# Layer 3 of a four-layer kernel: the next batch's group norm one step earlier, and keys' means between those of the first queries

## What is computed

```python
qkv = silu(x @ w_qkv.T)                     # q, k, v, each 8 heads of 32
q = rope(rms_norm(q, w_qn)); k = rope(rms_norm(k, w_kn))
wp = silu(x @ w_wp.T + b_wp)                # a width and a sharpness per head and position
scores = q . k over a 7x7 window * scale    # k and v zero-padded
soft_mask = sigmoid((width - rel_dist) * sharp)
attn = softmax(scores - (1 - soft_mask) * 10000)
out = rms_norm(sum(attn * v_window), w_on)
return silu((out + v) @ w_out.T)
```

## Time and profile before

| | us |
|---|---|
| median of 3 runs | 3466.73 (3464.69 to 3476.52) |
| the profiled execution, whole time | 3469.34 |
| its span on the core | 3467.5 |
| TensorE matmul busy | 3105.6 (90% of the span) |
| VectorE busy | 2211.7 (64%) |
| ScalarE busy | 2058.1 (59%) |
| GpSimd busy | 1155.1 (33%) |

### The profile page before, as it was taken

How to read it: one execution, slowest core, us unless ns; L and a number is a source line. 1 busy time by engine, 2 the same in 40 slices (tenths; PEclk the granted TensorE clock), 3 DMA queues, 4 the chain that set the end, 5 groups by cost and what they waited for, 6 DMA issues and landing times. The chain is left out here.

```text
span 3467.5 us, 94027 instructions
## 1 busy us (share of the span) xinstructions
PE 3105.6 (90%) x38656; PEld 1750.2 (50%) x38656; DVE 2211.7 (64%) x5202; ACT 2058.1 (59%) x4412; POOL 1155.1 (33%) x1446
## 2 busy tenths in 40 slices
PE   6999999999955999999999858999994899999996
PEld 2333333333312556566656526777772566666664
DVE  5878878887733667676777533545543566666765
ACT  2667676767633555545555515656562677777774
POOL 3433434343301222222222202222222455555554
PEclk9999999999976999999999979999997999999998
DMA  6777787777852333323323214445443233333332
GB/s 201 155 173 164 157 184 173 152 174 160 170 130 68 66 86 84 83 72 86 84 71 72 74 57 139 145 143 159 145 133 128 67 93 107 107 113 113 110 95 83
DMA packets 286233, 413.94 MB, mean 119 GB/s; under 512 B 25952, under 2 KB 242800, under 8 KB 264816
## 3 DMA queue, kind: packets, MB, share of 16 engines
q1 hardware_dynamic: 263248, 270.32, 26.0%
q0 software_dynamic: 18432, 134.23, 19.4%
q10 hardware_dynamic: 4128, 3.39, 0.3%
HBM read 219.30 MB, written 53.81 MB: 79 GB/s over the span
## 5 line engine op out<-in xcount | busy, mean ns | idle before, releaser
L732 DVE TENSOR_TENSOR l_probs<-l_psum,l_decay 128x1024 f32<-128x1024 f32 x512 | 598.6, 1219 | 163.5 <-PE l_psum L628 152.8
L780 ACT ACTIVATE l_sizes<-l_probs 128x2048 f32<-128x2048 f32 x256 | 487.6, 1910 | 300.3 <-DVE l_probs L732 293.0
L1793 ACT ACTIVATE l_logits<-l_logits,l_low 128x100 f32<-128x100 f32 x1024 | 374.7, 369 | 238.1 <-DVE l_low L1773 237.1
L1800 POOL TENSOR_TENSOR l_logits<-l_logits,l_inv 128x400 f32<-128x400 f32 x256 | 235.0, 918 | 737.7 <-DVE l_inv L1779 736.8
L628 PE MATMUL l_psum<-l_qk 32*128 32x512 f32 x2048 | 340.6, 646 | 7.9 <-POOL l_qk L866 4.2
L881 POOL DMA_DIRECT2D l_sizes<-l_sizes x128 | 111.5, 871 | 548.1 <-ACT l_sizes L780 536.1
L1632 POOL TENSOR_TENSOR l_E<-l_E,l_causal 128x1024 f32<-128x1024 f32 x64 | 153.3, 2396 | 378.0 <-DVE l_x_act L1365 224.8
L643 PE MATMUL l_psum<-l_probs,l_V 128*32 128x512 f32 x2048 | 270.6, 600 | 1.7 <-DVE l_probs L732 1.6
L299 PE MATMUL l_psum<-l_xT,l_w_up 128*128 128x512 f32 x512 | 232.2, 607 | 12.7 <-DVE l_row_var L1423 8.6
L1735 PE MATMUL l_psum<-l_keys,l_q_blocks 128*64 128x100 f32 x4096 | 230.6, 253 | 3.7 <-issue 2.4
L2726 POOL TENSOR_SCALAR l_soft<-l_dist,l_sharp,l_border 128x100 f32<-128x100 f32 x512 | 229.0, 464 | 0.1
(11 more groups left out here) (246 smaller groups left out, 6072.0 us busy)
## 6 DMA issues: line engine op xcount, KB each, us to landing
l_sizes<-l_sizes POOLq DMA_DIRECT2D x128, 1024.0 KB, 7.5
l_V_windows<-v_image SPq DMA_DIRECT2D x512, 100.0 KB
l_V_windows<-v_padded SPq DMA_DIRECT2D x512, 100.0 KB
l_E<-rows_c SPq DMA_DIRECT2D x64, 512.0 KB, 5.8
l_xT<-y SPq DMA_DIRECT2D x24, 1024.0 KB, 5.3
y<-l_res SPq DMA_DIRECT2D x32, 512.0 KB, 3.7
l_e_everywhere<-rows_e SPq DMA_DIRECT2D x112, 128.0 KB, 5.6
l_xT<-x SPq DMA_DIRECT2D x8, 1024.0 KB, 11.7
```

The lines of the kernel that those rows point to most:

```text
L732: nc.vector.tensor_tensor(probs[:, N % 2, 2 * p:2 * p + 2, :], ring.region(name).rearrange("p (a n) -> p a n", a=2), decay[:, h:h + 2, s0: ...
L780: nc.scalar.activation(sizes[:, slot(N), :, :], probs[:, N % 2, :, :], ACT.Abs).then_inc(sized, 1)
L1793: nc.scalar.activation(e, e, ACT.Exp, scale=-1.0, bias=self.low[:, N % 4, i:i + 1], accum_out=self.total[:, N % 4, i:i + 1]).then_inc(self ...
L1800: nc.gpsimd.tensor_tensor(p, p, self.inv[:, N % 4, :].unsqueeze(2).to_broadcast([P, STEP, NKEY]), ALU.mult).then_inc(self.p_ready, 1)
```

## The change

- In `MEANS` the first key's mean comes between those of the first two queries, and a table `MEAN_OF` tells where a unit's mean is. VectorE scales key 0 in step 13 instead of 14, key 1 in step 14 instead of 15, keys 2 and 3 in step 15 as before; query 1 is scaled in step 14 as before.
- `bn_stats` of the first half of batch b+2 run in step 15 of batch b, ahead of that step's keys (those of batch b+1 were in step 0). Those of the second half and the combining are in step 0 (were in step 1). For the first transition, all of it is in step 0.
- The group average, its copy, the variance and the root are in step 1 (were in step 2). In the ring, `("gn", b + 1)` thus stands ahead of the last values' transpose.
- GpSimd applies the norm in step 2 (was step 3), again behind that step's scaling.

```diff
-MEANS = (("q", 0, 0), ("q", 0, 1), ("k", 0), ("k", 1), ("k", 2), ("k", 3), ("q", 1, 0), ("q", 1, 1))
+MEANS = (("q", 0, 0), ("k", 0), ("q", 0, 1), ("k", 1), ("k", 2), ("k", 3), ("q", 1, 0), ("q", 1, 1))
+MEAN_OF = {("q", u): (0, 2, 6, 7)[u] for u in range(4)} | {("k", u): (1, 3, 4, 5)[u] for u in range(4)}
-KEYS_AT = {14: (0, 1), 15: (1, 4)}
+KEYS_AT = {13: (0, 1), 14: (1, 2), 15: (2, 4)}
...
-            if n == 2 and b + 1 < B:
+            if n == 1 and b + 1 < B:
                 order.append(("gn", b + 1))
...
-                    if n == 2 and b + 1 < B:
+                    if n == 1 and b + 1 < B:
                         norm.average(nc, pe, ring, b + 1)
...
-                    if n < 2 and b + 1 < B:
-                        norm.moments_of(nc, dve, b + 1, n)
+                    if n == 15 and b + 2 < B:
+                        norm.moments_of(nc, dve, b + 2, 0)
+                    if n == 0 and b + 1 < B:
+                        if b == 0:
+                            norm.moments_of(nc, dve, 1, 0)
+                        norm.moments_of(nc, dve, b + 1, 1)
+                        norm.combine(nc, dve, vstep)
                     if n == 1 and b + 1 < B:
-                        norm.combine(nc, dve, vstep)
-                    if n == 2 and b + 1 < B:
                         norm.collect(nc, dve, ring, b + 1)
...
-                            scale_query(b + 1, n - 13)
+                            scale_query(b + 1, 2 * (n - 13))
...
-                    if n == 2 and b + 1 < B:
+                    if n == 1 and b + 1 < B:
                         norm.root(nc, act, b + 1)
...
-                    if b + 1 < B and n == 2:
+                    if b + 1 < B and n == 1:
                         norm.variance(nc, pool, pstep, ring, b + 1)
                     if b + 1 < B:
-                        if n == 3:
+                        if n == 2:
                             apply(b + 1)
```

More of the change, by code:

```diff
@@ L2142 @@
 SQUARES_AT = {10: (0, 2), 11: (2, 3), 12: (3, 4), 13: (4, 6), 14: (6, 8)}
-KEYS_AT = {14: (0, 1), 15: (1, 4)}
+KEYS_AT = {13: (0, 1), 14: (1, 2), 15: (2, 4)}
 def number_of(j):
-    return j - 2 if MEANS[j][0] == "k" else j if j < 2 else j - 4
+    return sum(MEANS[i][0] == MEANS[j][0] for i in range(j))
 def unit_name(unit, b):
@@ L2474, in scale_key @@
                     g, half = u % 2, u // 2
-                    dve.wait_ge(r_ready, 8 * b + u + 3)
+                    j = MEAN_OF["k", u]
+                    dve.wait_ge(r_ready, 8 * b + j + 1)
                     r0 = WIN // 2 + 16 * half
                     k = keys[b % 2][:, g, :].rearrange("p (r c) -> p r c", c=IMAGE)[:, r0:r0 + 16, WIN // 2:WIN // 2 + SIDE]
-                    nc.vector.scalar_tensor_tensor(k, k, w_qk[:, 0:1], rec[:, (u + 2) % 4, :].rearrange("p (r c) -> p r c", c=SIDE),
+                    nc.vector.scalar_tensor_tensor(k, k, w_qk[:, 0:1], rec[:, j % 4, :].rearrange("p (r c) -> p r c", c=SIDE),
                                                    ALU.mult, ALU.mult).then_inc(k_done, 1)
```

## The result

The changed kernel takes 3490.22 us (median of 12 runs, 3477.44 to 3494.43) beside 3471.41 us for the kernel before in the same comparison (12 runs, 3455.25 to 3485.89): a ratio of 1.0050, with a 95% interval of 1.0031 to 1.0069. That is slower by 0.5%, some 17 to 19 us. The forecast was 3479.5 us, 12.8 above the median then known (3466.73).

The account below looks back on a forecast made before the run. TensorE, busy 92 of 100 us, bounds the kernel, so the change acts only through its stalls. Six steady transitions at 1.8 us plus 1.7 for the first give 12.5 us more: 3479.5 us, range 3464 to 3491.

Parts of the forecast that it names:

- the main case: The whole kernel slower through the added stalls, 3475 to 3486 us; chance 0.62.
- the case with the clock: Rival: two stalls within 7 us lower TensorE's clock, 1.8 to 3 us more a transition, about 3497 us; chance 0.08.
- Item 1: VectorE's interleaved keys, steps 13 to 15: same work up to step 0, cost and gain 0.
- Item 2: First bn_stats pair ahead of step 15's keys: TensorE's stall before step 0's scores grows from 0.47 to 1.7, +1.2 us.
- Items 3 and 4: Steps 0 and 1: VectorE's scores start later; the group average waits 1.9 us for ScalarE's copy of a value transpose.
- Items 5 and 6: From the average to step 4: +2.6 us at the outputs' mean, +1.8 at the step-4 units without the norm's wait.
- item 5: From the average to the outputs' mean (L2381): 6.74 us of TensorE work, ScalarE ends last at 2921.8; shift +2.6 us.
- Item 7: GpSimd's scaling for step 4's turn, now behind the apply: just in time, price 0; starved, up to 0.8 us late.
- The first transition: No keys to delay, but both pairs and the combining precede step 1's scores: step-4 units +1.7 us.
- Half of it swallowed: Rival: the step-5 stall on the values takes back half of the shift, leaving 6 us, 3473 us; chance 0.23.

Follow-up runs that it names:

- e1: The kernel before with the interleaved order of means and keys alone: six batch periods 545.29 us, against 545.03 before.
- e2: The kernel before with only the first bn_stats pair moved to step 15, ahead of the keys: six periods 552.26 us, against 545.03 before.
- e4: The changed kernel with TensorE's group average at the end of step 1, behind turn and weighing: six periods 547.55 us, against 560.44.
- e3: The changed kernel with the bn_stats pair of step 15 behind that step's keys instead of ahead: six periods 554.81 us, against 560.44.
- e6: The changed kernel with GpSimd's apply of the norm back in step 3: six periods 570.19 us, against 560.44.
- e9: The kernel before with bn_stats pairs at the end of step 15 and in step 0, two query scalings moved to steps 5 and 6: ratio 1.0015 to the kernel before.
- e10: The changed kernel with bn_stats behind the keys, average behind the weighing, two query scalings in steps 5 and 6: ratio 1.0047 to the kernel before.
- e5: The changed kernel with bn_stats behind the keys and average behind the weighing: six periods 540.08 and 542.06 us, ratio 1.0009 to the kernel before.

## Why the prediction was right, and where it was off

The direction and the mechanism were right, the size was too small. The measured 3490.22 us lie inside the range of 3464 to 3491, but by less than 1 us, and above the main case's own 3475 to 3486. Part of that gap is the base: the kernel before had a median of 3471.41 in the comparison, 4.7 above the one the forecast was added to. That the range held was partly luck, since it had been drawn to leave out the case with the clock.

**Item 1, keys at no cost:** right as far as one trace can tell (e1).

**Item 2, +1.2 us for the pair:** right. 1.71 us at step 0 for a forecast of 1.7, and 7.2 us over six periods by itself (e2).

**Items 3 and 4, the added wait:** right in place and size: 1.86 us at L398 for 1.9, released by the copy of the first transpose; e4 shows it by removal.

**Items 5 and 6, +1.8 us at step 4:** right as a balance of stalls. Over the six periods L1729 gained 7.4 us (3.35 to 10.71) and L398 8.8 (2.38 to 11.19), the norm gave 4.3 and the copy and squares of the outputs together about 1: +10.8 or so, that is 1.8 in each of six. **What failed is the work in item 5.** It carries the 6.74 us of work from the turn to L2381 over as if TensorE kept its full clock. In the transition shown, L2382 starts 15.3 us after the scores of step 0, where items 2 to 5 give 14.2 (2907.6 to 2921.8), and the step-4 units 19.4 instead of 18.6: 0.8 us more in the transition. In six the measured 15.4 contain 4.6 us beyond those stalls. TensorE's busy time alone grew by 6.4 us; other waits shrank, so that its idle time grew by 9.0 and not by 10.8. The clock's fall stood among the rivals, as an alternative with 0.08 and 1.8 to 3 us a transition. It came together with the main case, in most transitions, at some 0.8 us each, and it does not need the two stalls together, as that rival had it (e3). The argument against it was the 0.98 of the earlier trace rows; but that is a mean over 100 us, and it holds a fall to 0.66 over 5 us behind the 1.87 us stall in step 5 of the same kernel. Read in short windows, the trace of before had shown that a stall of this length can bring the clock down.

**Item 7:** the starved scaling did not happen. The one behind the apply took 1.29 us beside the query instead of 0.85, and TensorE's wait on it stayed at 1.7 us in six. e6 shows the other side, which the item did not price: given the late average, putting the apply back in step 3 costs 9.8 us.

**The first transition, +1.7:** 1.66 measured.

**Half of it swallowed:** fell. The step-5 stall is 1.9 us a batch before and after: it moved with the step-4 units. What sets its length is another matter, since in e9 and e10, where the queries are scaled elsewhere, it is gone.

**Not foreseen:** the rest after the seventh transition is 2.05 us longer. Even e1, whose edit costs nothing in the six periods, has 174.64 there, so this part of the difference of two traces is not shown to be the change's.

## What to carry to other kernels

Before moving a step forward, look at what its engine does just there: 1.2 us ahead of late keys cost 1.2 us a batch, and the same 1.2 us behind them nothing. A unit moved in a ring also moves its wait: here the new neighbour's release hung on work of the same step, and putting the small matmul behind two that were ready took most of the wait away. And count a stall's effect on the clock along with the stall.

## What the runs showed of the hardware

- TensorE's clock. In 13 of 18 cases it fell to the lower of its two levels (1.2 of 2.4 GHz) at a stall of 1.8 to 2.3 us before the average, and was full again 3 to 4 us later, in three cases 7. With 0.6 to 0.8 us at that place (e4) it stayed full. It took no stall of 5 or 6 us, like those of the kernel before's first and last batch. One kernel had two falls in one trace and five in another at the same stall (e5). Why the same stall brings it down in some batches and not in others was not tried.
- GpSimd beside VectorE. VectorE's scaling of a query or a key, which reads two tensors in SBUF, slows what GpSimd does: the apply 3.01 to 4.74 us, twelve mask arguments 4.92 to 9.74 us. `bn_stats`, which reads one, did not: a scaling took 0.85 us beside it. The Trainium skill (SBUF — State Buffer, "SBUF: two separate sides") names such a pair of ports and says that the one that starts first holds it for the whole instruction. That the two are in each other's way agrees with these rows. That the first holds on does not fit the scaling of the earlier trace rows, which began 0.4 us ahead of three keys, took 3.19 us and left the keys undelayed, unless the start that the profile shows comes before the ports are granted, which no run here can tell.
